# Choosing experts inside the end of the attention: one Trainium2 core, attention and a mixture of experts

## What is computed

```python
x = x + layernorm(attention(layernorm(x), Wq, Wk, Wv, Wo))      # 16 heads of 16, causal, rotary
h = layernorm(x)                                                # 2048 rows of 256
probs = softmax(h @ gate_w.T)                                   # 16 experts
topk_w, topk_idx = top_k(probs, 4)
topk_w = topk_w / topk_w.sum(-1)
shared = (silu(h @ sg) * (h @ su)) @ shared_down.T              # inner width 704
shared = shared * sigmoid(h @ shared_gate_vec.T)
sparse = sum over the 16 experts of (silu(h @ g_e) * (h @ u_e)) @ down_e.T * weight_e   # inner width 176
x = x + layernorm(shared + sparse)
```

## Time and profile before

| | us |
|---|---|
| median of 3 runs | 621.13 |
| lowest, highest | 619.58, 626.93 |
| the profiled execution | 622.44 |
| its span | 620.7 |
| TensorE busy | 523.1 (84%) |
| VectorE busy | 408.0 (66%) |
| ScalarE busy | 342.7 (55%) |
| GpSimd busy | 325.9 (53%) |

### The profile page before, as it was taken

One profiled execution on the slowest core, in us unless ns is written; L12 is line 12 of the kernel. 1 busy time (PEld: TensorE's weight loads), 2 busy tenths in 40 slices (PEclk: granted clock), 3 DMA queues, 4 the chain that ended last, 5 costly groups with the idle time before them and its releaser, 6 DMA issues.

```text
span 620.7 us, 11606 instructions
## 1 busy us (share of the span) xinstructions
PE 523.1 (84%) x3550; PEld 401.6 (65%) x3550; DVE 408.0 (66%) x1005; ACT 342.7 (55%) x701; POOL 325.9 (53%) x357
## 2 busy tenths in 40 slices
PE   2737899899999998878887886968999999999573
PEld 1624455656565453356666775857999999999452
DVE  6539878888788857249735644635997666665337
ACT  2241576696578558655442315535887666666314
POOL 5431543481464215215276566624778887777624
PEclk9859899999999999989897988987999999999878
DMA  7231661535063440340036323439998888887595
GB/s 271 74 129 52 194 192 46 168 128 155 21 216 104 132 136 2 101 141 2 9 138 214 119 81 123 164 125 256 230 248 164 147 150 141 138 134 108 68 343 199
DMA packets 71034, 86.34 MB, mean 139 GB/s; under 512 B 6272, under 2 KB 64192, under 8 KB 70976
## 3 DMA queue, kind: packets, MB, share of 16 engines
q1 hardware_dynamic: 53264, 63.15, 32.3%
q0 software_dynamic: 14448, 19.31, 18.0%
q10 hardware_dynamic: 3264, 3.15, 1.5%
HBM read 33.68 MB, written 39.12 MB: 117 GB/s over the span
## 4 chain that ended last, share of the span: by engine, by line
PE 35%; DVE 8%; issue 4%; DMA 3%; ACT 3%; another core or an unknown queue 2%; POOL 1%; ACTq 0%; POOLq 0%; SPq 0%; DVEq 0%
PE gate_ps L1953 12%; PE y_ps L1976 7%; PE y_ps L1929 3%; PE m_ps L1871 3%; PE gate_ps L939 2%; PE up_ps L939 2%; PE up_ps L1964 1%; PE up_ps L1965 1%; DVE hid L1677 1%; PE gate_ps L1985 1%; DVE hid_lo L1707 1%; ACT yst L1393 1%; DMA added<-acc_dram 1%; PE up_ps L1985 1%
## 5 line engine op out<-in xcount | busy, mean ns | idle before, releaser
L1288 POOL DMA_INDIRECT acc_dram<-yout,xin x79 | 125.5, 1588 | 54.4 <-ACT yout L1421 26.7
L703 DVE TENSOR_REDUCE nmax<-a_ps 128x2 f32<-128x768 f32 (+3 forms) x88 | 96.0, 1119 | 13.7 <-PE a_ps L838 13.2
L588 ACT ACTIVATE probs<-a_ps 128x1024 f32<-128x1024 f32 (+1 forms) x96 | 81.3, 883 | 29.2 <-PE a_ps L860 25.2
L489 POOL TENSOR_SCALAR_AFFINE_SELECT probs<-probs 128x256 f32<-128x256 f32 (+1 forms) x96 | 47.1, 501 | 92.3 <-ACT probs L588 92.2
L1276 POOL DMA_INDIRECT xs_dram<-xrow,idx x64 | 66.3, 1037 | 43.4 <-issue 27.0
L1953 PE MATMUL gate_ps<-w_all,rxT_hi 128*128 x316 | 78.2, 330 | 1.6 <-issue 0.9
L1755 DVE TENSOR_TENSOR h<-rsilu,gate_ps 128x176 f32<-128x176 f32 x79 | 26.6, 337 | 51.8 <-ACT rsilu L1406 40.9
L1976 PE MATMUL y_ps<-w_all,hT_hi 128*128 x237 | 58.0, 313 | 0.3 <-DVE hT_lo L1762 0.2
L1953 PEld LDWEIGHTS gate_ps<-w_all,rxT_hi 128*128 128x128 f32 x316 | 53.0, 192 | 3.2 <-issue 3.0
L833 PE MATMUL a_ps<-KTt,QT 96*128 96x128 bf16 (+3 forms) x256 | 50.3, 307 | 4.6 <-DVE nmax L703 2.2
L860 PE MATMUL a_ps<-QT,KTt 99*128 99x512 bf16 (+3 forms) x256 | 47.8, 301 | 4.7 <-DMA QT<-nT 1.8
(11 more groups left out here) (315 smaller groups left out, 1372.0 us busy)
## 6 DMA issues: line engine op xcount, KB each, us to landing
xin<-xs_dram SPq DMA_DIRECT2D x79, 136.5 KB
xs_dram<-zeros SPq DMA_DIRECT2D x7, 1365.0 KB, 6.6
w_all<-in_wex_dram SPq DMA_DIRECT2D x16, 480.0 KB
QT<-parts SPq DMA_DIRECT2D x48, 128.0 KB
KTt<-parts SPq DMA_DIRECT2D x48, 128.0 KB
acc_dram<-zeros SPq DMA_DIRECT2D x6, 640.0 KB, 8.1
added<-acc_dram ACTq DMA_DIRECT2D x12, 256.0 KB, 9.3
x_all<-in_x_dram SPq DMA_DIRECT2D x4, 512.0 KB, 7.3
```

Source lines behind the costliest of these rows:

```text
L489: pool.affine_select(out=pr, in_=pr, pattern=[[0, nh], [1, P]], compare_op=ALU.is_ge, fill=0.0, base=0, channel_multiplier=-1).then_inc(ma ...
L588: nc.scalar.activation(dst, src, ACT.Exp, scale=float(DH) ** -0.5).then_inc(a_act, 1)
L703: nc.vector.tensor_reduce(nmax[:, i, h:h + nh].rearrange("p (b h) -> p b h", h=hb), src, AX.X, ALU.max, negate=True).then_inc(a_dve, 1)
L1288: pool.indirect_dma_start(out=acc[a][:, :], out_offset=bass.IndirectOffsetOnAxis(ap=xin[:, p % XIN, XROW - 1:XROW].bitcast(mybir.dt.uint32 ...
```

## The change

Routing and combination of three batches (12 tiles) are emitted as new items at the head of T_ORDER; PARTS becomes tiles 0 to 11 and 12 to 15. The functions exponentials, route and combination move to module level, their tiles to places that are free in that segment, and the zeroing of count becomes the item zero of GpSimd. Their instructions are otherwise the same. ranks(0) comes at step 0 instead of 1, and the first slots one step earlier. Both turn_in and rows_high of the first two pages move behind the last step. SyncE asks for twelve pages, then stores the shared result, then asks for experts 5, 6 and 7, and for the others at pages 16, 18 and so on. The splits of experts 5 to 15 shift by four pages (SPLIT), and page p waits for p // 3 + 1 experts. The pace of the scatters changes.

```diff
-PACE_FROM = 7
+PACE_FROM = 8
 TAILS = 3
+SPLIT = 4
+PARTS = (slice(0, NT - TB), slice(NT - TB, NT))
 T_ORDER = [
-    ("score", 2, 0), ("score", 2, 1), ("score", 2, 2), ("score", 2, 3), ("score", 2, 4), ("pv", 2, 0),
+    ("route",), ("score", 2, 0), ("zero",), ("score", 2, 1), ("exps",), ("route",), ("route",), ("route",), ("route",),
+    ("route",), ("combine",), ("score", 2, 2), ("score", 2, 3), ("score", 2, 4), ("pv", 2, 0),
...
+                elif kind == "zero":
+                    pool.memset(t["count"][:], 0.0).then_inc(t["count_zeroed"], 1)
...
+                elif kind == "exps":
+                    exponentials(nc, act, t, 0)
...
+                elif kind == "route":
+                    dve.wait_ge(a_dve, seg.past.at("aD", ("lturn",)))
+                    next(routing)
+                elif kind == "combine":
+                    next(combining)
...
-        RANK0, TURN_L, RANK1, TABLE = 1, 5, 10, 14
+        RANK0, TURN_L, RANK1, TABLE = 0, 5, 10, 14
...
-            for q in range(PAGES):
+            def load_page(q):
+
                 if q >= XIN:
                     sp.wait_ge(y_added[(q - XIN) % ACCS], 16 * ((q - XIN) // ACCS + 1))
                 sp.dma_start(xin[:, q % XIN, :], xs[q * P:(q + 1) * P, :]).then_inc(xin_in[q % XIN], 16)
...
+            for q in range(XIN):
+                load_page(q)
+            store_shared(B - 1)
+            sp.wait_ge(down_done, NSTEP)
+            sp.wait_ge(tab_ready, 1)
+            for i in range(2):
+                sp.wait_ge(ysh_stored[i], 16 * (B // 2))
+            for k in range(early, early + TAILS):
+                expert(k)
+            for q in range(XIN, PAGES):
+                load_page(q)
+                k = early + TAILS + (q - SPLIT - XIN) // 2
+                if q >= SPLIT + XIN and (q - SPLIT) % 2 == 0 and k < E:
                     expert(k)
...
-                        step, event = divmod(PACE_FROM + n * 15 // 16, 3)
+                        step, event = divmod(PACE_FROM + n * 7 // 8, 3)
...
-                if n == NSTEP - 1:
-                    rows_high(0)
-                    rows_high(1)
...
+            rows_high(0)
+            rows_high(1)
...
-                if p >= 2 and early + (p - 2) // 2 < E:
-                    if p % 2 == 0:
-                        expert_high(early + (p - 2) // 2)
+                k = early + (p - SPLIT - 2) // 2
+                if p >= SPLIT + 2 and k < E:
+                    if (p - SPLIT) % 2 == 0:
+                        expert_high(k)
...
-            plan = {0: [routing, routing], 1: [mixing], 2: [slots0, combining], 3: [slots0, slots0], 4: [slots0],
-                    5: [routing_last, slots0], 7: [routing_last, routing_last], 8: [routing_last, routing_last],
+            plan = {1: [mixing], 2: [slots0, slots0], 3: [slots0, slots0], 4: [slots0],
+                    5: [routing_last], 7: [routing_last, routing_last], 8: [routing_last, routing_last],
...
-                if n == NSTEP - 1:
-                    turn_in(0)
-                    turn_in(1)
...
+            turn_in(0)
+            turn_in(1)
...
-                    pe.wait_ge(w_ready, min(E, p // 2 + 1))
+                    pe.wait_ge(w_ready, min(E, p // 3 + 1))
```

More of the change, by code:

```diff
@@ L34 @@
 PACE = 2
-PACE_FROM = 7
+PACE_FROM = 8
 TAILS = 3
+SPLIT = 4
+ROUTED = ("eprob", "prob", "count", "more", "same", "crest", "comb", "mask16", "top", "big")
+PARTS = (slice(0, NT - TB), slice(NT - TB, NT))
 ZPAGES, ZACC, ZEROS = 10, 5, 17
@@ L940, in products, with exponentials, linked, link @@
     return ins
+def exponentials(nc, act, t, part):
+    o = PARTS[part]
+    logit, eprob = t["logit"], t["eprob"]
+    act.wait_ge(t["centred"], part + 1)
+    nc.scalar.activation(eprob[:, o, E:GC], logit[:, o, E:GC], ACT.Exp, scale=-1.0).then_inc(t["exp_ready"], 1)
+    nc.scalar.activation(eprob[:, o, 0:E], eprob[:, o, 0:E], ACT.Exp).then_inc(t["exp_ready"], 1)
+def linked(dve, t):
+    def link(ins):
+        t["links"] += 1
+        ins.then_inc(t["step_done"], 1)
+        dve.wait_ge(t["step_done"], t["links"])
+    return link
@@ new lines, in combination, with over @@
+def combination(nc, t, link, part):
+    xrow = t["xrow"]
+    prob, more, crest, big = t["prob"], t["more"], t["crest"], t["big"]
+    o = PARTS[part]
+    wide = [P, o.stop - o.start, E]
+    def over(ap):
+        return ap.unsqueeze(2).to_broadcast(wide)
+    link(nc.vector.tensor_tensor(crest[:, o, 0:E], more[:, o], prob[:, o], ALU.mult))
+    link(nc.vector.tensor_reduce(big[:, 0, o], crest[:, o, 0:E], AX.X, ALU.add))
+    link(nc.vector.reciprocal(big[:, 1, o], big[:, 0, o]))
+    link(nc.vector.tensor_tensor(xrow[:, o, D:D + E], crest[:, o, 0:E], over(big[:, 1, o]), ALU.mult))
+    yield
@@ L1499, in combination @@
-            def combination(part):
-                o = PARTS[part]
-                wide = [P, o.stop - o.start, E]
-                def over(ap):
-                    return ap.unsqueeze(2).to_broadcast(wide)
-                link(nc.vector.tensor_tensor(crest[:, o, 0:E], more[:, o], prob[:, o], ALU.mult))
-                link(nc.vector.tensor_reduce(big[:, 0, o], crest[:, o, 0:E], AX.X, ALU.add))
-                link(nc.vector.reciprocal(big[:, 1, o], big[:, 0, o]))
-                link(nc.vector.tensor_tensor(xrow[:, o, D:D + E], crest[:, o, 0:E], over(big[:, 1, o]), ALU.mult))
-                yield
+            link = linked(dve, t)
@@ L1853, in ranks @@
                 n = o.stop - o.start
-                pe.wait_ge(mask_ready, part + 1)
+                pe.wait_ge(t["mask_ready"], part + 1)
                 pe.wait_ge(cst_in_sem, 32)
```

193 lines of the change are left out of this document (89 added, 104 removed).

## The result

The changed kernel took 618.56 us (median of 20 runs, 615.57 to 625.27), beside 622.36 us for the kernel before (median of 20). The ratio is 0.9945, with a 95% interval of 0.9922 to 0.9967: 3.4 us faster, where the prediction had 10. (The ratio leaves out the few slow runs, those over 1.5% above the fastest of their kernel, which is why it isn't the quotient of the two medians.) The time lies in the range that was given, near its slow end. The profiled execution took 617.46 us (span 615.7), 5.0 us less than the profiled one of before.

The account below looks back on a forecast made before the run. Pages bound by TensorE (2.04 us each), unchanged by the diff; gains sought in the last attention segment, shared steps and passage. +1.0 - 1.1 - 1.5 - 8.5 = -10.1 from 622.44 (612.3, or 611.0 by the median): forecast 611.5 us, range 606 to 617.

Parts of the forecast that it names:

- part 5: Passage from shared steps to pages: page 0 starts 2.8 us earlier, 6.0 us of waits and slow clock go; -8.5 us.
- experts late: Rival, pages: loads from expert 8 on wait for page additions, 2.27 to 2.72 us a page; slower, 624 us, chance 0.05.
- part 4: Scatters before the pages: last one 4 us earlier, near 402, so rows 0 and 1 are in SBUF by 407.
- Part 2: First shared steps: routing work leaves VectorE, hid_lo(1) then waits for ScalarE's hid_hi(1); -1.1 us, ends 0 and -3.
- Part 1: Last attention segment: routing of 12 tiles there mostly hidden, VectorE and GpSimd delaying each other; +1.0 us, at most 3.9.
- Part 3: Shared steps 8, 10 and 13: last batch of 4 tiles shortens VectorE's work, 0.5 us each; -1.5 us, ends 0 and -3.
- The pauses go too: Rival, shared steps: half of the unknown queue's 2% (6 us) happens to fall away; 605 us, chance 0.13.
- The passage gives half: Rival: rows no earlier, contention in the last segment at its upper end, experts from 8 on cost 1 us; 617, chance 0.17.
- It doesn't do what it says: Rival: scatters still end after 406, ScalarE still stands before expert 5, only parts 2 and 3 remain; 619 us, chance 0.05.

Follow-up runs that it names:

- ask_2_earlier: Kernel after with every expert from 8 on asked for two pages earlier, casts unchanged; 613.86 us, ratio 0.9858 to the kernel before.
- third_page: Kernel after with experts asked for and split at every third page instead of every second; 614.01 us, ratio 0.9873 to the kernel before.
- passage_ask_2: passage_alone with experts 8 to 15 asked for two pages earlier; 621.69 us, ratio 0.9987 to the kernel before.
- passage_alone: Kernel before with only the passage changed (load order, turns and row parts behind last step, later splits); routing, parts, pace as before; 624.92 us, ratio 1.0074.
- routing_alone: Kernel after with load order, splits, turns and rows_high as before; routing in the segment, parts of 12 and 4, new pace kept; 615.92 us, ratio 0.9888.
- parts_alone: Kernel before with parts of 12 and 4 tiles instead of 8 and 8, routing still between the shared steps; 626.2 us, ratio 1.0048.
- ask_2_turns_ahead: ask_2_earlier with turns and row parts of pages 0 and 1 back ahead of the last down product; 613.27 us, ratio 0.9859 to the kernel before.
- pace_alone: Kernel before with only the new scatter pace, parts of 8 and 8, routing and passage as before; 623.25 us, ratio 1.002.
- maxima_5x: Kernel after with the 12 maxima in the last attention segment done five times over; 621.63 us, ratio 0.9986 to the kernel before.
- third_turns_ahead: third_page with turns and row parts of pages 0 and 1 back ahead of the last down product; 612.33 us, ratio 0.984 to the kernel before.
- pace_before: Kernel after with the old scatter pace; 619.23 us, ratio 0.9948 to the kernel before.
- after_again: Kernel after, unchanged, run again for a second trace; 618.42 us, ratio 0.992 to the kernel before.

## Why the prediction was right or wrong

**The step that failed is part 5: it puts the wait for the experts behind the seventh at nothing.** The sum gave -8.5 for the passage and stopped at page 9. It let the same SyncE order, which asks for expert k only behind page 2k - 12's addition, run on for free. It cost 5.8 us between pages 12 and 28. The mechanism stood in the prediction as the rival "experts late", priced by its rates of 2.27 and 2.72 us a page over 17 pages at 3.9 to 11.6 us, with a chance of 0.05 and as a slower case. The price covers what was measured, and the chance was too low. The prediction's own figures spoke for the rival: it needed 18.1 us between a page's start and the cast eight pages later, and eight pages at 2.04 are only 16.3. I argued that away as the worst addition of a crowded stretch. What counted was how long before ScalarE's need the ask could go out: 1.8 us for expert 9, against a load that took 4.07. This is shown by ask_2_earlier, which moves the ask alone (ratio 0.9858 against 0.9945), borne out by third_page (0.9873), and shown again by passage_ask_2 against passage_alone (0.9987 against 1.0074). It accounts for 4.5 to 5.4 of the 6.7 us by which the forecast gain was too large.

**Part 5, -2.8 for page 0:** 3.0 us were measured (10.2 to 7.2), but for another reason. I gave it to the down product standing ahead of the turns. passage_alone has that order and gains 0.3; routing_alone has the old order and gains 5.3. The rows were there in time, which was part 4. With rows in time, the new order costs 2.3 us in the traces (7.2 in ask_2_earlier against 4.9 in routing_alone, both at a granted clock of 1.00 and with the first load some 0.5 us before the last hid). The timed pairs with the old order put back don't show that cost.

**Part 5, -6.0 for expert 5's wait:** right in mechanism. The wait is gone, TensorE is busy 24.36 of 24.40 us between page 0 and page 12, and the clock in this stretch was 0.93, where the start of the pages had 0.85 before. The gain was 4.6 us, and 6.1 in the same code run again, whose clock was 1.00 here. In the first trace 1.1 of it came with routing_alone, so some 3.5 us belong to the passage's new order. The prediction named only one of two waits there. Beside ScalarE's for expert 5, TensorE waited for the rows of page 6, whose load stood behind expert 5's in SyncE's queue (TensorE, kernel before):

```profile
424.33 0.48 PE L1871 MATMUL m_ps<-ident,xin 128*128 128x128 f32 x2 [1.98 <-DMA xin<-xs_dram]
```

The shift of the casts takes the first wait away, the twelve page loads asked for first the second. No run has one without the other.

**Part 4, rows 4 us earlier:** right in kind. The first scatter starts 4.1 us earlier and the last one 6.7, of which 3.9 are the earlier end of the shared steps; the first page load follows the last hid by 0.8 us instead of 3.4. So against the steps the last scatter gained 2.9 us and not 4. It isn't the parts alone (parts_alone 1.0048, first load at 2.8). Of nine traces with the routing in the segment and the larger part, eight had the first load between 2.6 us before and 2.1 us after the last hid; the ninth, ask_2_turns_ahead, had it at 3.6, in shared steps among the shortest. pace_alone had it at -0.1, in the longest. So whether rows are in time hangs on the length of the steps too, and the routing in the segment with parts of 8 and 8 wasn't tried: how the gain divides stays open.

**Part 2, -1.1:** steps 0 to 5 took 25.52 us before and 24.45 after: -1.07, and the same 24.4 to 24.5 in every kernel with the routing moved but maxima_5x (26.1), whose list was made longer. The reason was right too. hid_lo(1), in VectorE's timeline of the kernel after, waits for hid_hi as forecast; it waited for nothing but its own queue before:

```profile
287.84 0.69 DVE L1724 TENSOR_TENSOR hid_lo<-hid,hid_hi 128x512 fp32r<-128x512 f32 x1 [3.78 <-ACT hid_hi L1456]
```

Four microseconds of VectorE work taken out gave 1.1, because the next releaser was 1.1 us behind.

**Part 1, +1.0:** no cost above 0.5 us is seen. The segment, from the copy of the logits to the last low part, took 17.2 us, where it took 17.6 before and 16.7 in passage_alone, which has no routing in it. The 0.5 lies in the four transposes ahead of the segment's end, which took 1.11 us against 0.66 there, at the lower clock level (0.51 granted from 268.8 to 270.0 us, in passage_alone 0.96 from 267 to 271). The list ran from 255.21 to 266.41, 1.0 us later than the 265.4 that I worked out. Two comparisons and the last product took 0.79, 0.78 and 0.73 us, where a comparison of the same shape beside them took 0.36; GpSimd's selects ran at the same time. The Trainium skill (SBUF — State Buffer, "SBUF: two separate sides") says that a VectorE operation with two inputs in SBUF and a GpSimd operation that reads SBUF block each other, the one that comes later until the other's instruction is over. These rows agree with it in kind. Its price here was a list about 1.2 us longer, and 0.92 us of idle time were still left ahead of norm 3.

**Part 3, -1.5 for steps 8 to 13:** open. Steps 5 to 23 took from 93.6 to 108.9 us in these kernels, and single pauses without a known cause make up much of the spread. A gain of 1.5 us cannot be read from that. But the two groups differ: the five kernels with the routing between the steps took 97.3 to 108.9 us, 102.6 in the mean, and the nine traces with it moved 93.6 to 101.1, 97.5 in the mean. So this stage may have gained more than I forecast. The ranges overlap, and no run separates it from chance.

**The sum, put right:** -1.1 in steps 0 to 5 and -1.8 from the last hid to page 28 make -2.9, where the runs show -3.4. The same sum over the other kernels gives -7.4 for routing_alone (measured -7.0), -8.9 for ask_2_earlier (-8.8) and -8.0 for third_page (-7.9). For third_turns_ahead it gives -9.0 (-10.0). It is off for passage_alone (+2.8 against +4.6), passage_ask_2 (-4.7 against -0.8), parts_alone (+0.6 against +3.0), pace_before (-1.2 against -3.2) and after_again (-1.8 against -5.0), and far off for ask_2_turns_ahead (-2.0 against -8.8) and pace_alone (-5.3 against +1.2). So a single trace can be wrong by 7 us about what a kernel is worth: it shows which waits there are, and the timed runs show the worth. The misses have a pattern. The four other kernels with the routing between the steps were all slower than their sums, and the eight traces with it moved were faster than theirs or within 0.5 us. That would fit a gain in steps 5 to 23, which the sum leaves out, but it doesn't show one.

**The other rivals.** "The pauses go too" can't be told from chance: steps 5 to 23 were 3.7 us shorter in the profiled execution of after than in that of before, and in other kernels with the same steps anything between 0.5 us longer (101.1) and 7 us shorter (93.6). "The passage gives half" was among the nearest in its time (617; the measured ratio on the forecast's base of 621.13 gives 617.7, and the last case had 619), and one of its three terms, experts from 8 on, was real at six times its size; rows did come early and the segment cost next to nothing. "It doesn't do what it says" fell with the cast at 422.35, which waits for nothing.

## What to carry to other kernels

Where a queue asks for data behind a buffer's release, work out the distance from ask to use for the *last* member of the series and not the first. Moving the uses of a series moves its asks too, if they are written against the same index. When a change has two halves, price and try each alone. Here the half that was aimed at the visible wait of 3.4 us was a loss alone, and the other half alone had a better median than both together. And where work is taken off an engine that looks full, look for the releaser next in line: it decides the gain, not the work removed.

## What was unexpected of the hardware

The adding transfers of a page that lie on the kernel after's chain landed 3.7 to 7.1 us after their issue, in a stretch in which experts were loaded too. Everything chained behind one of them inherits that spread. Whether the loads cause it was not tested.

The second is a group of stalls in the shared steps that no releaser of the profile explains, and whose length differs between executions of the same code. The longest pieces of the chain between 300 and 400 us, in the kernel after (first fence) and in the same code run again (second):

```profile
316.91 6.48 issue
...
342.12 4.20 another core or an unknown queue
...
363.92 6.37 another core or an unknown queue
```

```profile
317.49 5.54 issue
...
341.33 3.98 another core or an unknown queue
...
366.20 4.23 another core or an unknown queue
```

The longest single one is in pace_alone (parts_alone has one of 16.43 us at 321.19, passage_ask_2 one of 14.20 at 320.03):

```profile
319.04 16.41 another core or an unknown queue
```

Steps 5 to 23 took 96.9 us in the kernel after, 93.6 us in the same code run again, and 108.9 us in pace_alone. The pauses near 317, 342 and 365 us come back in about the same places with other lengths. What they are isn't settled here. They hide a change of a few microseconds in this stage.
